# The list of expert units beside the last scatters, expert constants and weights ahead, and a last normalisation that holds the whole residual

## The reference

```python
logits = x @ gate.T                       # 64 experts
idx, w = route(sigmoid(logits) + bias)    # 4 of 8 groups, then the best 8 experts of a token
w = w / (w.sum(-1) + 1e-20) * 2.5
# up to CAP = 512 tokens of each expert, in the order of the tokens:
h  = silu(xe @ w1[e]) * (xe @ w3[e])      # 512 -> 256
ye = h @ w2[e]                            # 256 -> 512
out = sum over a token's experts of w * ye
shared = silu(x @ sg.T) * (x @ su.T) @ sd.T
x = layernorm(x + out + shared)           # mean and variance over 512, eps 1e-5
```

## Time and profile before

| What | us |
|---|---|
| Median of 3 runs | 3575.05 |
| Lowest and highest run | 3569.9 and 3582.3 |
| The profiled execution, its own time | 3602.69 |
| Its span, first to last instruction | 3600.6 |
| Mean granted TensorE clock | 0.948 of full |

### The profile page before, as it was taken

One profiled execution on the slowest core, in us unless ns is written; L12 is line 12 of the kernel. 1 busy time (PEld: TensorE's weight loads), 2 busy tenths in 40 slices (PEclk: granted clock), 3 DMA queues, 4 the chain that ended last, 5 costly groups with the idle time before them and its releaser, 6 DMA issues. The chain is left out here.

```text
span 3600.6 us, 63650 instructions
## 1 busy us (share of the span) xinstructions
PE 3158.3 (88%) x18557; PEld 2032.8 (56%) x18557; DVE 2176.4 (60%) x4841; ACT 1384.8 (38%) x3155; POOL 1552.0 (43%) x1110
## 2 busy tenths in 40 slices
PE   7998999989899998989797999997988882999990
PEld 4444444444544444444345777775766771888880
DVE  3645546465554645556354888885666663777775
ACT  1443434434354443534322666664000001444441
POOL 3352434424244342434532333332566664566661
PEclk8999989999999999999998999998999996999995
DMA  4122121222203222021273112211221112899996
GB/s 116 44 68 72 33 69 40 68 72 53 73 15 85 56 68 72 21 68 60 87 253 139 59 62 66 62 62 62 62 53 53 53 50 85 240 253 252 248 254 210
DMA packets 189188, 343.99 MB, mean 96 GB/s; under 512 B 36137, under 2 KB 54698, under 8 KB 187946
## 3 DMA queue, kind: packets, MB, share of 16 engines
q1 hardware_dynamic: 132778, 242.51, 23.3%
q0 software_dynamic: 28800, 48.43, 6.0%
q10 hardware_dynamic: 27392, 50.34, 3.8%
HBM read 206.96 MB, written 83.89 MB: 81 GB/s over the span
## 5 line engine op out<-in xcount | busy, mean ns | idle before, releaser
L553 ACT ACTIVATE sa_probs<-sa_s 128x512 f32<-128x512 f32 (+3 forms) x1280 | 614.9, 537 | 740.6 <-PE sa_s L444 410.8
L338 POOL TENSOR_TENSOR sa_both<-sa_probs 128x2048 f32<-128x2048 f32 (+2 forms) x160 | 589.9, 3687 | 683.3 <-PE sa_pv L471 671.7
L410 PE MATMUL sa_w<-sa_parts 96*128 96x512 f32 (+3 forms) x1280 | 516.5, 454 | 114.8 <-DVE sa_pmax L612 36.1
L444 PE MATMUL sa_s<-sa_parts 128*128 128x512 f32 (+3 forms) x1280 | 458.6, 409 | 18.9 <-ACT sa_probs L553 13.6
L616 DVE TENSOR_REDUCE sa_pmax<-sa_w 128x1 f32<-128x512 f32 (+3 forms) x768 | 419.3, 584 | 86.1 <-PE sa_w L410 82.8
L410 PEld LDWEIGHTS sa_w<-sa_parts 96*128 96x128 f32 x1280 | 236.4, 195 | 407.2 <-DVE sa_pmax L612 120.8
L612 DVE CUSTOM_DVE_ANT_0 sa_w<-sa_w,sa_maskS 128x512 f32<-128x512 f32 (+3 forms) x512 | 326.3, 649 | 227.5 <-PE sa_w L410 220.9
L444 PEld LDWEIGHTS sa_s<-sa_parts 128*128 128x128 f32 x1280 | 243.6, 195 | 130.5 <-ACT sa_probs L553 64.4
L1409 POOL DMA_INDIRECT token_and_weight_of_slot<-rt_entry,rt_sl x256 | 254.6, 995 | 144.7 <-issue 74.8
L462 PE MATMUL sa_pv<-sa_probs,sa_values 128*32 128x512 f32 (+3 forms) x2560 | 274.4, 547 | 0.0
L1230 ACT ACTIVATE xa_sm<-xa_sm,xa_nmax 128x154 f32<-128x154 f32 x512 | 208.8, 410 | 72.4 <-DVE xa_nmax L1162 72.4
(11 more groups left out here) (234 smaller groups left out, 5767.6 us busy)
## 6 DMA issues: line engine op xcount, KB each, us to landing
ex_w<-in_w SPq DMA_DIRECT2D x138, 512.0 KB
sa_parts<-early_halves SPq DMA_DIRECT2D x384, 128.0 KB, 2.5
early_xt<-in_xT SPq DMA_DIRECT2D x32, 1024.0 KB, 5.6
scratch_attention_T<-sa_oT SPq DMA_DIRECT2D x32, 256.0 KB, 2.1
on_at<-scratch_attention_T SPq DMA_DIRECT2D x32, 256.0 KB, 3.2
on_xr<-in_x SPq DMA_DIRECT2D x32, 256.0 KB
scratch_x<-on_xn ACTq DMA_DIRECT2D x32, 256.0 KB, 2.1
scratch_x_T<-on_xnT ACTq DMA_DIRECT2D x32, 256.0 KB, 3.3
```

The lines of the kernel that those rows point to most:

```text
L338: pool.tensor_tensor(both[:, :, 0:w], probs[:, even, :, 0:w], probs[:, odd, :, 0:w], ALU.add).then_inc(both_ready, 1)
L410: nc.tensor.matmul(ps[:, 0:w], qparts[0:3 * HD, h, q0:q0 + P], kparts[0:3 * HD, h, k0:k0 + w], start=True, stop=True).then_inc(work_ready, 1)
L444: mm = nc.tensor.matmul(ps[:, 0:w], kparts[:, h, kb * P:(kb + 1) * P], qparts[:, h, q0:q0 + w], start=True, stop=not diag)
L553: nc.scalar.activation(probs[:, r % NPB, h, 0:w], sbank[n % NSB][:, 0:w], ACT.Exp).then_inc(exp_done, 1)
```

## The change

What was a block of its own is taken into the routing block. A small class `Lists` holds what outlives the stage: the list, the table's entries, the identity, the three weight buffers and their semaphores. The index vectors and the zeros are made by GpSimd with routing's other constants, as are the list's cleared memory, the identity and the four transfers into `unused`. TensorE's sum goes into the bank `gps` behind the last tile. VectorE makes the list in the last tile, before it waits for `oh`. SyncE brings the list from SBUF to SBUF, without DRAM, loads the first unit's weights, waits for all scatters and then issues the load of the entries, all before the barrier. The unit loop itself stays as it was.

`last_norm` holds all 16 pairs at once, issues all 16 loads without a wait, gives the second half of each pair to GpSimd, and is written out instead of looped. A partition now holds two neighbouring rows of a pair, 4 KB in one piece.

```diff
+class Lists:
+...
+    def load_weights(self, sp, e, s):
+        for dst, src in ((self.w1, self.w1T), (self.w3, self.w3T), (self.w2, self.w2T)):
+            sp.dma_start(dst[:, s], src[e]).then_inc(self.w_in[s], 16)
...
                 each_tile(sp, body)
                 sp.wait_ge(spare_set, 32)
+                sp.wait_ge(worklist_done, 1)
+                sp.wait_ge(lists.set_up, 1)
+                sp.dma_start(lists.worklist[0:1, 0:2 * UNITS].rearrange("o (u c) -> o u c", c=2), wli[:]).then_inc(lists.worklist_in, 16)
+                sp.wait_ge(lists.worklist_in, 16)
+                first = sp.value_load(lists.worklist[0:1, 0:1], min_val=0, max_val=UNITS - 1) // UPE
+                lists.load_weights(sp, first, 0)
+                for s in range(2):
+                    sp.wait_ge(scat[s], 128 * (NT // 2))
+                sp.dma_start(lists.entries[:].rearrange("p n e c -> p n (e c)"),
+                             table.rearrange("(n p e) c -> p n (e c)", p=P, e=E_)).then_inc(lists.entries_in, 16)
...
+                step(pool.iota(iou[:], pattern=[[1, UNITS]], base=0, channel_multiplier=0))
+                step(pool.iota(row[:], pattern=[[0, 1]], base=1, channel_multiplier=1))
+                step(pool.memset(zrow[:], 0.0))
                 pool.sem_inc(consts, 1)
+                step(pool.memset(lists.worklist[:], 0))
...
+                for n in range(2 * J):
+                    pool.dma_start(unused[n], lists.zero[:]).then_inc(lists.added, 16)
...
                 each_tile(pe, body)
+                pe.wait_ge(cum_done, NT)
+                pe.wait_ge(sc_done, NT)
+                nc.tensor.matmul(gps[:, 0:E_], ones[:], cum[:, NT % 2], start=True, stop=True).then_inc(tot_done, 1)
...
                     step(dve.reciprocal(wrec[:], wrec[:]))
+                    if isinstance(t, int) and t == NT - 1:
+                        list_units()
                     dve.wait_ge(oh_done, t + 1)
...
-        with nc.Block() as block:
-...
 def last_norm(nc, sems, res, out):
...
         def rows(dram, t):
-            return dram[bass.ds(t * (PAIR * P), PAIR * P), :].rearrange("(n p) d -> p n d", p=P)
+            return dram[t * (PAIR * P):(t + 1) * (PAIR * P), :].rearrange("(p n) d -> p n d", p=P)
...
+            for t in range(PAIRS):
+                sp.dma_start(r[:, t], rows(res, t)).then_inc(r_in[t], 16)
...
+            for t in range(PAIRS):
+                pool.wait_ge(rstd_done, t + 1)
+                apart(pool, passed)
+                pool.tensor_scalar(r[:, t, 1], r[:, t, 1], mv[:, t, 1, 0:1], rstd[:, t, 1:2], ALU.subtract,
+                                   ALU.mult).then_inc(second_done, 1)
```

More of the change, by code:

```diff
@@ L1296, with __init__, sb, route_and_shared @@
 SPARE = UNIT
-def route_and_shared(nc, sems, x2, x2T, early, gateT, ebias, res, table, worklist):
+AHEAD = 2
+COLS = CAP // P
+J = UNIT // P
+class Lists:
+    def __init__(self, nc, ctx, w1T, w3T, w2T):
+        def sb(name, shape, dt=F32):
+            return ctx.enter_context(nc.sbuf_tensor("list_" + name, shape, dt))
+        self.w1T, self.w3T, self.w2T = w1T, w3T, w2T
+        self.worklist = sb("worklist", [1, 2 * (UNITS + AHEAD)], I32)
+        self.entries = sb("entries", [P, COLS, E_, 2])
+        self.identf = sb("identf", [P, P])
+        self.zero = sb("zero", [P, 1])
+        self.w1 = sb("w1", [P, 2, KT, FF])
+        self.w3 = sb("w3", [P, 2, KT, FF])
+        self.w2 = sb("w2", [P, 2, FF // P, DM])
+        self.set_up = kept_semaphore(nc, ctx, "list_set_up")
+        self.worklist_in = kept_semaphore(nc, ctx, "list_worklist_in")
+        self.entries_in = kept_semaphore(nc, ctx, "list_entries_in")
+        self.w_in = [kept_semaphore(nc, ctx, f"list_w_in{i}") for i in range(2)]
+        self.added = kept_semaphore(nc, ctx, "list_added")
+    def load_weights(self, sp, e, s):
+        for dst, src in ((self.w1, self.w1T), (self.w3, self.w3T), (self.w2, self.w2T)):
+            sp.dma_start(dst[:, s], src[e]).then_inc(self.w_in[s], 16)
+def route_and_shared(nc, sems, x2, x2T, early, gateT, ebias, res, table, unused, lists):
     with ExitStack() as ctx:
@@ L1577, in locate, with list_units, step @@
                     dve.wait_ge(w8_done, t + 1)
+                def list_units():
+                    n = 0
+                    def step(ins):
+                        nonlocal n
+                        n += 1
+                        ins.then_inc(lstep, 1)
+                        dve.wait_ge(lstep, n)
+                    step(dve.tensor_copy(iouf[:], iou[:]))
+                    step(dve.tensor_copy(rowf[:], row[:]))
+                    dve.wait_ge(tot_done, 1)
+                    step(dve.tensor_copy(tot[:], gps[:, 0:E_]))
+                    av = actv[:].rearrange("p (e u) -> p e u", u=UPE)
+                    for u in range(UPE):
+                        step(dve.tensor_scalar(av[:, :, u], tot[:], float(u * UNIT), None, ALU.is_gt))
+                    step(dve.tensor_tensor_scan(incl[:], actv[:], zrow[:], 0.0, ALU.add, ALU.add))
+                    step(dve.tensor_scalar(hot[:], incl[:], rowf[:], None, ALU.is_equal))
+                    step(dve.tensor_tensor(hot[:], hot[:], actv[:], ALU.mult))
+                    step(dve.tensor_tensor_reduce(out=hot[:], in0=hot[:], in1=iouf[:], scale=1.0, scalar=0.0, op0=ALU.mult,
+                                                  op1=ALU.add, accum_out=wl[:, 0:1]))
+                    step(dve.tensor_copy(wl[:, 1:2], incl[:, UNITS - 1:UNITS]))
+                    dve.tensor_copy(wli[:], wl[:]).then_inc(worklist_done, 1)
                 def finish(t, s):
@@ L1646, in experts @@
-def experts(nc, sems, x2, table, worklist, w1T, w3T, w2T, res, unused):
-    J = UNIT // P
+def experts(nc, sems, x2, lists, res):
     FT = FF // P
@@ L1657, in ps @@
             return ctx.enter_context(nc.psum_tensor("ex_" + name, [P, 512], F32))
-        AHEAD = 2
-        COLS = CAP // P
         TERMS = ((0, 0), (0, 1), (1, 0))
         BUNDLE = 8
[L1662 to L1666, removed]
+        wl, entries, identf = lists.worklist, lists.entries, lists.identf
+        w1, w3, w2 = lists.w1, lists.w3, lists.w2
+        token = sb("token", [P, E_ * COLS], I32); weight = sb("weight", [P, E_ * COLS])
         w1h = sb("w1h", [P, 2, 2, KT, FF], F32R); w3h = sb("w3h", [P, 2, 2, KT, FF], F32R); w2h = sb("w2h", [P, 2, 2, FT, DM], F32R)
@@ L1937, in last_norm @@
     PAIR = 2
[L1938 to L1939 removed]
+    PAIRS = NT // PAIR
     with ExitStack() as ctx:
```

121 lines of the change are left out of this document (50 added, 71 removed).

## The result

| | Before | After |
|---|---|---|
| Median of 4 runs | 3577.95 us | 3543.88 us |
| Lowest and highest | 3569.9 and 3582.3 | 3541.77 and 3550.51 |
| Span of the profiled execution | 3600.6 | 3543.5 |

The ratio is 0.9913 (0.9899 to 0.9927), 31 us less at the 3577.95 of before (26 to 36). The forecast was 3539, in a range from 3522 to 3557. It was taken from the 3575.05 of three runs; a fourth has moved the median of before up by 2.9 us, so the forecast gain of 36.4 would now give 3541.6. For the same reason the profiled execution's own time was 3545.2 and not the 3566.3 of my sum.

What follows compares the result with a forecast made beforehand. The experts are bound by TensorE; the change touches two stretches where TensorE does nothing. The seam's 17.7 us and the last normalisation's 18.7 sum to 36.4, taken off 3575.05 for 3538.6 us, range 3522 to 3557.

Steps and rivals of the forecast that it cites:

- Last scatter's issue to the stage's start: Seam, end of routing: with the list made earlier, the experts start 6.3 us earlier, bounds 5.9 to 7.7.
- Gather's landing: Seam, end of the second gather's issue to TensorE's use of its rows: 4.1 us instead of 5.4, a gain of 1.3.
- Last normalisation: Final stage: takes 46 us instead of 64.7, 18.7 less, with bounds of 43 and 53.
- The list at no cost: Seam: VectorE's 3.05 us of list instructions cost nothing in routing's last tile, where VectorE idles 8.51 us for `oh`.
- Rival E: Seam: the list isn't ready when SyncE needs it and scatters are late; about 20 us gained, 3555; chance 0.05.
- The wait for `added`: Expert stage's start: taking this wait off, less the entries that replace it, brings the first source copy 10.1 us earlier.
- The last normalisation by its transfers, 45.9: Final stage: 42.2 us of full transfer work, 1.7 before the first data and 2.0 for the last landing; ends last.
- rival A: Last normalisation: transfers stay at 371 GB/s, reads and writes together; 15.7 us less there, 3541.6; chance 0.13.
- VectorE's side of it, 44.4: Last normalisation: first statistics after 4.5 us, a period of 2.15 us per pair, 44.4 us in all.
- GpSimd's half: Last normalisation: GpSimd's normalising instruction takes 0.65 to 1.3 us each, beside VectorE's statistics, no bound.
- Rival D: Last normalisation: GpSimd becomes the bound, slower than before from 4.4 us an instruction; 3585 at 5 us; chance 0.02.
- Rival B: Last normalisation: VectorE and GpSimd take turns, adding 0.65 us per pair, 3546.8, or 1.3 each, 3556.6; chance 0.10.

Runs made afterwards that it cites:

- late_added: Changed kernel with the four transfers into `unused` issued in the expert stage again; one run of 3595.20 us beside 3606.33 for the kernel before.
- hold_unit2: Changed kernel with the load of unit 2's weights (counted from 0) held until unit 0's rows are transposed; 3540.78 us, ratio 0.9895.
- norm_act_hold: Changed kernel with ScalarE normalising both halves, GpSimd none, and unit 2's weights held until unit 0's rows are transposed; 3539.81 us, ratio 0.9888.
- norm_2k_rows: Changed kernel with the last normalisation's rows laid out as before, in pieces of 2 KB; one run of 3577.96 us beside 3606.33 for the kernel before.
- norm_immediates: Changed kernel with GpSimd's half subtracting 0.0 and multiplying by 1.0, leaving the second tile of each pair not normalised; one run, 3541.25 us.
- before_again: The kernel before, unaltered, run once more for a second trace; 3578.01 against 3576.24 us, ratio 1.0005.
- late_weights: Changed kernel with the first unit's weights loaded in the expert stage, behind the barrier; one run of 3589.83 us beside 3606.33 for the kernel before.
- norm_both_dve: Changed kernel with both halves of each pair normalised by VectorE, none by GpSimd; one run of 3576.53 us beside 3606.33 for the kernel before.

## Why the prediction was right

Direction, range and the two places were right, and the sum was 4.6 us too high: 31.8 us measured in the stretches, 36.4 forecast. That 3543.9 stands against 3539 is close to the same difference by luck, since the median of before moved up by 2.9 and the medians lie 34.1 apart, 2.3 more than the stretches. The stage's start is taken at SyncE's last step out of the barrier, 3022.88 before and 2991.02 now. Step by step, forecast gain against measured:

| Step | Forecast | Measured |
|---|---|---|
| Last scatter's issue to the stage's start | 6.3 | 13.43 - 6.77 = 6.7 |
| Stage's start to the first source copy | 10.1 | 12.74 - 2.92 = 9.8 |
| Copy to the second gather's end | 0 | 3.44 - 3.69 = -0.2 |
| Gather's landing | 1.3 | 5.38 - 5.97 = -0.6 |
| Last normalisation | 18.7 | 64.72 - 48.61 = 16.1 |

- The list at no cost: right. VectorE made it from 2964.91 to 2968.12 and then still waited 5.19 us for `oh`. Rival E is out.
- The wait for `added`: right, and late_added shows its size, 9.0 us.
- The gather, "It now meets one unit's weights instead of two": wrong, and the mis-sized term of the seam. Six transfers leave from 2993.36 to 2998.10, around the gathers' issue, which ends at 2997.63, again two units' worth: the first unit's weights are split by 2996.6, 7 us before the first transposes, as I wrote, and I didn't ask what their free buffer sets off. hold_unit2 shows it: 3.49 us of landing without them, inside my bounds (3 to 5.4), against 5.97 with them, outside.
- The last normalisation by its transfers, 45.9: a bound of the right size, but not the one that ends last. norm_act_hold, where the transfers are full up to 3534, takes 46.3. The rate was forecast as that of weight loads, 426 GB/s, and came out at 419 for loads and stores mixed; by this rival A is out. The reason given for it failed, though: rows of 2 KB reach 407 (norm_2k_rows), so larger rows are worth 3% in the full stretches and not the 15% between 371 and 426, and 0.7 us in the stage. The page SBUF — State Buffer of the Trainium skill, section Summary: rules for kernel authors, gives about 358 GB/s; the trace disagrees, at 419.
- VectorE's side of it, 44.4, is what ended last, at 48.6, and the term that failed in it is GpSimd's half, "so 0.65 to 1.3 us each, beside VectorE's statistics, no bound". It takes 2.07 us with VectorE idle and 2.23 beside it. It cost twice. First the period: 2.22 instead of 2.15, 0.8 us at the last statistics (37.6 instead of 36.8); norm_immediates, with 2.15 again, shows that GpSimd is the reason. Then the tail: behind the last statistics I had 7.6 us, it took 11.0, since the last GpSimd half ends at 3538.75, 3.3 us after the reciprocal where VectorE's half needs 0.6. 44.4 + 0.8 + 3.4 = 48.6. GpSimd is busy without a pause and so has no room left, but 2.2 us is about VectorE's own pace, and so it cost these 4 us and not 16 times 1.
- Rival D named this danger, a GpSimd dearer than its neighbours. Its price was not reached: it put the kernel slower than before from 4.4 us an instruction on. A copy of the same shape (610 ns) is no neighbour of an instruction with two operations: it said a quarter of what was found.
- Rival B, VectorE and GpSimd in each other's way, is there too, but small: VectorE's half takes 0.62 us instead of 0.545, about 1 us in all, none of the 0.65 each. The Trainium skill, page SBUF — State Buffer, section Who interferes with whom, calls the shared port an exclusive lock that is held for the whole instruction; it says so of scalar instructions when VectorE runs them in a two-port mode, and no run here shows the mode. If this instruction is one of them, the trace disagrees. VectorE's last half runs from 3535.48 to 3536.03, 0.55 us, inside a GpSimd instruction that began before it and ended at 3536.69:

```profile
3534.46 2.23 POOL L1972 TENSOR_SCALAR ln_r<-ln_r,ln_mv,ln_rstd 128x512 f32<-128x512 f32 x1
```

  Held to its end it would have taken over 1.2 us. The 0.07 is lost only by the 14 halves during which, some 0.34 us after their start, one GpSimd instruction ends and the next begins; in norm_immediates this falls 0.17 us after their start and costs nothing. Why these 0.17 us matter stays open.

## What to carry to other kernels

Where a wait is taken off the path, follow the engine that it frees: buffers that come free early send the next load, and that load meets the one transfer on which the start hangs. Give a half of the work to another engine only with a row of the same operation and width on it; a copy's row says nothing of it. And when a ring of buffers is opened, price the ring (here 12 to 13 us), the engine's period and the transfers apart, since what is won is set by the one that ends last once the ring is gone, and the last item's way through the slowest engine is paid in full.

## What the runs showed of the hardware

- Routing takes 462 to 465 us in some executions and 496 to 508 in others, with the same kernel. The groups view of the kernel before, in its first profile:

```profile
L1430 PE MATMUL rt_gg<-rt_xT,early_xt 128*128 128x128 f32 x1024 | 139.9, 285 | 40.1 <-issue 39.8
L1430 PE MATMUL rt_uu<-rt_xT,early_xt 128*128 128x128 f32 x1024 | 134.2, 289 | 15.3 <-issue 15.0
```

and of before_again:

```profile
L1430 PE MATMUL rt_gg<-rt_xT,early_xt 128*128 128x128 f32 x1024 | 127.4, 285 | 0.0
L1430 PE MATMUL rt_uu<-rt_xT,early_xt 128*128 128x128 f32 x1024 | 119.6, 275 | 0.0
```

  TensorE stands still for 54.8 us with nothing that the profile shows as a cause, and the stage is 34.3 us longer, at a granted clock of 0.94 against 0.95 of before_again. late_added, late_weights, norm_both_dve and norm_2k_rows, which ran one after the other, all show it, and the run of the kernel before beside them took 3606.33 us; no other profile but the first shows it. These four ran on another chip than the other experiments; the record doesn't say which chip the first profile is from. So it goes with the session or the chip and not with the kernel, and it is why stretches are compared here and not spans. What causes it stays open.
- Four small transfers of GpSimd, the last issued by 3033.91 in late_added, let SyncE go on only at 3041.53, 7.6 us later (7.2 in the kernel before).
- GpSimd's two-operation instruction at 128x512 takes 2.07 us with VectorE idle and 2.23 beside it (1.92 and 2.17 with its two numbers given in the instruction), ScalarE's with scale and bias 0.80, VectorE's 0.545.
- The first gathers land late beside weight loads: 5.4 to 6.5 us from the end of the second gather's issue to the first transposes with two units' weights in flight, 3.3 and 3.5 with one (hold_unit2, norm_act_hold).
- Full transfers reached 419 GB/s with loads and stores mixed at rows of 4 KB, and 407 at 2 KB, in the same 18 us of the stage.
